# Folding constant as four 32-row products, rings of 4, and the 64-unit product on two column groups

## What is computed

```python
k = key_param @ Wk + bk ; v = k @ Wv + bv            # 32 patterns only
A = sparsemax((query @ Wq + bq) . k / sqrt(32))      # per head, over 32 patterns
attn = transpose(A @ v, (0, 2, 1, 3)).reshape(B, L, H*D) @ Wo + bo
x = layernorm(query + attn)
s = x @ Win + bin_                                   # 512 -> 64
h = relu(s[..., None] * W1 + b1)                     # 64 x 16
g = einsum('btmh,mh->btm', h, W2) + b2
x = layernorm(x + g @ Wout + bout)
```

## Time and profile before

| | us |
|---|---|
| median of 3 runs | 1581.36 (1575.73 to 1583.24) |
| the profiled execution | 1570.85 |
| its span, first to last instruction | 1569.1 |
| PE busy in the span | 1415.4 (90%) |
| ACT busy | 1105.0 (70%) |
| DVE busy | 1096.9 (70%) |
| POOL busy | 655.8 (42%) |
| mean share of PE's full clock granted | 0.96 |

### The profile page before, as it was taken

The page is one execution under the profiler, slowest core; times in us unless marked ns, Lnnn a source line. Parts: engine busy times, 40 slices in busy tenths (PEclk is TensorE's granted clock), DMA queues, the critical chain, the costliest instruction groups (busy, mean ns, idle before and its releaser), DMA issues. The chain is left out here.

```text
span 1569.1 us, 25895 instructions
## 1 busy us (share of the span) xinstructions
PE 1415.4 (90%) x6102; PEld 915.1 (58%) x6102; DVE 1096.9 (70%) x4547; ACT 1105.0 (70%) x2402; POOL 655.8 (42%) x1645
## 2 busy tenths in 40 slices
PE   6887388799999999999999999999999999889984
PEld 5444144466666666666666666666666666545542
DVE  2654754578877877878788777888778777834454
ACT  3443143367787887788887787878888878867784
POOL 1221022223454444545544554444544444544444
PEclk9998698899999999999999999999999999989995
DMA  4333033655555555455545555555545555446753
GB/s 133 124 104 97 27 108 108 187 183 162 169 189 189 186 179 177 165 189 189 188 157 174 189 172 172 176 189 189 182 174 177 175 189 189 162 162 232 251 157 72
DMA packets 91798, 258.50 MB, mean 165 GB/s; under 512 B 15651, under 2 KB 15651, under 8 KB 75206
## 3 DMA queue, kind: packets, MB, share of 16 engines
q1 hardware_dynamic: 91590, 256.39, 49.0%
HBM read 206.00 MB, written 50.33 MB: 163 GB/s over the span
## 5 line engine op out<-in xcount | busy, mean ns | idle before, releaser
L610 PE MATMUL bank<-G_sb,pT 128*128 128x512 f32 x1024 | 465.7, 598 | 0.0
L977 DVE MAX8 top<-bank 128x8 f32<-128x32 f32 x2048 | 212.5, 181 | 146.9 <-issue 124.3
L610 PEld LDWEIGHTS bank<-G_sb,pT 128*128 128x128 f32 x1024 | 186.7, 192 | 186.9 <-issue 186.9
L419 POOL TENSOR_TENSOR shift_sq<-sum,per_row_sq 128x1 f32<-128x1 f32 x256 | 99.8, 390 | 413.1 <-DVE y_sb L883 412.8
L1019 DVE SCALAR_TENSOR_TENSOR acc<-hinge,w2c,acc 128x512 f32<-128x512 f32 x224 | 167.3, 747 | 61.3 <-ACT hinge L721 54.3
L721 ACT ACTIVATE hinge<-s_sb,b1c,w1c 128x512 f32<-128x512 f32 x256 | 205.7, 807 | 0.0
L706 ACT ACTIVATE unread<-y_sb,shift_sq 128x512 bf16<-128x512 f32 x256 | 183.1, 715 | 24.9 <-POOL minus_mean L421 24.8
L540 PE MATMUL bank<-A_hi,xT_hi 128*128 128x512 f32 x512 | 200.5, 392 | 0.0
L541 PE MATMUL bank<-A_lo,xT_hi 128*128 128x512 f32 x512 | 200.4, 391 | 0.0
L542 PE MATMUL bank<-A_hi,xT_lo 128*128 128x512 f32 x512 | 200.1, 391 | 0.0
L444 POOL TENSOR_TENSOR side<-side 128x256 bf16<-128x256 bf16 x128 | 86.6, 676 | 240.8 <-ACT side L793 240.8
(11 more groups left out here) (122 smaller groups left out, 2644.2 us busy)
## 6 DMA issues: line engine op xcount, KB each, us to landing
G_sb<-G_of_heads SPq DMA_DIRECT2D x128, 1024.0 KB, 5.4
x_sb<-in_L_attn_query_dram SPq DMA_DIRECT2D x128, 256.0 KB, 4.7
y_sb<-in_L_attn_query_dram SPq DMA_DIRECT2D x256, 128.0 KB, 5.4
out_dram<-o_sb SPq DMA_DIRECT2D x256, 128.0 KB, 4.7
G_of_heads<-y_sb SPq DMA_DIRECT2D x64, 256.0 KB, 2.6
y_sb<-in_L_attn_Wk_dram SPq DMA_DIRECT2D x1, 1024.0 KB, 5.6
y_sb<-in_L_attn_Wq_dram SPq DMA_DIRECT2D x1, 1024.0 KB, 8.2
y_sb<-in_L_attn_Wv_dram SPq DMA_DIRECT2D x1, 1024.0 KB
```

Source lines behind the costliest of these rows:

```text
L419: nc.gpsimd.tensor_tensor(shift_sq[:, par:par + 1], total[:, par:par + 1], per_row_sq[:], ALU.mult).then_inc(s_mean, 1)
L610: mm = nc.tensor.matmul(o_ps[i % 2][:], pT[:, bass.ds(pair_place(turn, i) + (i % H * C + c) * P, P)], G_sb[:, i % GR, c, :], start=(c == 0 ...
L977: mx = nc.vector.max(top8[:, h, :], z_ps[i % 2][:, h * S:(h + 1) * S])
```

## The change

1. `XR` and `OR`, the rings of `x_sb` and `o_sb`, go from 2 to 4 buffers.
2. The folded constant is built from `V_rep` instead of `V_blk`: each head's `v` repeated four times side by side, with no zeros around it. A unit of four pieces (a = 0 to 3) takes partitions 32a to 32a+31 of `VT_rep` and of `Wo_sb` and writes bank a: four 32-row matmuls, each on its own 32 rows of the array. A piece now serves four heads (32 of its 128 rows for each), so its store goes to four places in `G_dram`. There are four pieces to a slot, in slots 1 to 16, and one `bo` matmul for every sixteen pieces. In slot 0, 16 matmuls against 32 columns of the identity replace the 16 transposes, and one ACT copy the four. POOL loses two fills and the second fill of `first_place`.
3. The 64-unit product streams its 128 tokens as two halves of 64: for each chunk one product into partitions 0 to 63 (tokens 0 to 63) and one into partitions 64 to 127 (tokens 64 to 127) of the bank. ACT writes four 64 x 64 pieces instead of two of 64 x 128. `bin_sb` is loaded twice.

```diff
-        XR, YR, OR, UR, HR = 2, 16, 2, 8, 2
+        XR, YR, OR, UR, HR = 4, 16, 4, 8, 2
...
-            k = 3 * (turn * UNROLL + j - 1) if isinstance(turn, int) else PIECES
-            return range(max(k, 0), max(min(k + 3, PIECES), 0))
+            unit = turn * UNROLL + j - 1
+            return range(HPC * unit, HPC * unit + HPC) if 0 <= unit < PIECES // HPC else range(0)
...
                 for k in pieces(turn, j):
-                    h, c = k // C, k % C
+                    heads, c, a = piece(k)
                     sp.wait_ge(s_Gev, k + 1)
-                    sp.dma_start(G_dram[h, :, c * D:(c + 1) * D], y_sb[:, k % STAGES, :]).then_inc(
-                        s_Gst[k % STAGES], 16)
+                    sp.dma_start(G_dram[HPC * heads:HPC * heads + HPC, a * S:(a + 1) * S, c * D:(c + 1) * D],
+                                 y_sb[:, k % STAGES, :]).then_inc(s_Gst[k % STAGES], 16)
...
                     for c in range(C):
-                        mm = nc.tensor.matmul(ys_ps[0:M, 0:P], Win_sb[:, c, :], yT[:, c, :], start=(c == 0),
-                                              stop=(c == C - 1))
+                        for t in range(2):
+                            tokens = slice(t * HALF, (t + 1) * HALF)
+                            mm = nc.tensor.matmul(ys_ps[t * M:(t + 1) * M, 0:HALF], Win_sb[:, c, :],
+                                                  yT[:, c, tokens], start=(c == 0), stop=(c == C - 1))
...
-                    if c == 0:
-                        nc.tensor.matmul(G_ps[k % C][:], first_place[:], bo_row[:], start=True, stop=False)
-                    nc.tensor.matmul(G_ps[k % C][:], VT_blk[:, h, :], Wo_sb[:, c, :], start=(c > 0),
-                                     stop=True).then_inc(s_Gmm, 1)
+                    with_bo = c == 0 and a == 0
+                    if with_bo:
+                        nc.tensor.matmul(G_ps[a][:], ones_row, bo_row[:], start=True, stop=False)
+                    nc.tensor.matmul(G_ps[a][:], VT_rep[rows, heads * P:(heads + 1) * P], Wo_sb[rows, c, :],
+                                     start=not with_bo, stop=True).then_inc(s_Gmm, 1)
...
-                    for half in (slice(0, M), slice(M, P)):
-                        nc.scalar.activation(s_sb[half, par, q * P:(q + 1) * P], ys_ps[0:M, 0:P], ACT.Identity,
-                                             bias=bin_sb[:]).then_inc(s_sc, 1)
+                    for t in range(2):
+                        for half in (slice(0, M), slice(M, P)):
+                            rows = slice(t * M, (t + 1) * M)
+                            nc.scalar.activation(s_sb[half, par, q * P + t * HALF:q * P + (t + 1) * HALF],
+                                                 ys_ps[rows, 0:HALF], ACT.Identity,
+                                                 bias=bin_sb[rows, :]).then_inc(s_sc, 1)
```

More of the change, by code:

```diff
@@ L151, in build_kernel @@
         G_sb = sb("G_sb", [P, GR, C, D])
-        V_blk, VT_blk = (G_sb[:, r].rearrange("p c n -> p (c n)").rearrange("p (h n) -> p h n", h=H)
-                         for r in range(2))
+        V_rep, VT_rep = G_sb[:, 0].rearrange("p c n -> p (c n)"), G_sb[:, 1, 0, :]
         G_dram = nc.dram_tensor("G_of_heads", [H, P, C * D], F32, kind="Internal").ap()
@@ L158, in build_kernel @@
         bo_row = sb("bo_row", [1, D])
-        first_place = sb("first_place", [1, P])
+        ones_row = sb("ones_row", [1, P])[:]
         Win_sb = sb("Win_sb", [P, C, M])
@@ L163, in build_kernel @@
         bout_rows = sb("bout_rows", [P, D], F32R)
-        bin_sb = sb("bin_sb", [M, 1])
+        bin_sb = sb("bin_sb", [P, 1])
         w1c = sb("w1c", [P, KH])
@@ L288, in pieces, with piece @@
         def pieces(turn, j):
-            k = 3 * (turn * UNROLL + j - 1) if isinstance(turn, int) else PIECES
-            return range(max(k, 0), max(min(k + 3, PIECES), 0))
+            unit = turn * UNROLL + j - 1
+            return range(HPC * unit, HPC * unit + HPC) if 0 <= unit < PIECES // HPC else range(0)
+        def piece(k):
+            return k // (HPC * C), k // HPC % C, k % HPC
         def group_of(turn, i):
             return turn * (UNROLL // GROUP) + i // GROUP
-        KEY_LOADS, Q_LOADS, WLOADS = 3, 2, 16
-        FILLS = 15 + S
-        CONSTS = FILLS + 5
+        KEY_LOADS, Q_LOADS, WLOADS = 3, 2, 17
+        FILLS = 13 + S
+        CONSTS = FILLS + 4
         @block.sync
@@ L322, in _ @@
                     (Wout_sb[half, :], Wout),
+                    (bin_sb[half, :], bin_.rearrange("(m a) -> m a", a=1)),
                     (w1c[half, :], W1[:, j * KH:(j + 1) * KH]),
@@ L350, in slot @@
                     if isinstance(turn, int) and base + i < H:
-                        if h < GR:
+                        if h == 0:
                             sp.wait_ge(s_Gmm, PIECES)
-                        for k in range(C * h, C * h + C):
-                            sp.wait_ge(s_Gst[k % STAGES], 16 * (k // STAGES + 1))
+                        if h % HPC == 0:
+                            for r in range(STAGES):
+                                sp.wait_ge(s_Gst[r], 16 * (h // HPC + 1) * (HPC * C // STAGES))
                     if not isinstance(turn, int) or base + i >= GR:
@@ L592, in slot @@
                     if not isinstance(turn, int) or base + i >= 1:
-                        pe.wait_ge(s_sc, 2 * (base + i))
+                        pe.wait_ge(s_sc, 4 * (base + i))
                     for c in range(C):
@@ L635, in slot @@
                     nc.tensor.matmul(f_ps[:], acc_lo[:, here], Wout_hi[:], start=False, stop=True).then_inc(s_f, 1)
[L636 to L642, removed]
-                for k in pieces(turn, j):
-                    h, c = k // C, k % C
-                    if c == 0:
[L646 to L651, removed]
-                        nc.tensor.matmul(G_ps[k % C][:], first_place[:], bo_row[:], start=True, stop=False)
-                    nc.tensor.matmul(G_ps[k % C][:], VT_blk[:, h, :], Wo_sb[:, c, :], start=(c > 0),
-                                     stop=True).then_inc(s_Gmm, 1)
+                if turn == 0 and j == 0:
+                    for h in range(H):
+                        mm = nc.tensor.matmul(G_ps[0][:, h * S:(h + 1) * S],
+                                              V_rep[:, h * P:(h + 1) * P],
+                                              ident[:, 0:S], start=True, stop=True)
+                    mm.then_inc(s_vT, 1)
+                for k in pieces(turn, j):
+                    heads, c, a = piece(k)
+                    rows = slice(a * E, (a + 1) * E)
+                    pe.wait_ge(s_vTc, 1)
+                    if k >= HPC:
+                        pe.wait_ge(s_Gev, k - HPC + 1)
+                    with_bo = c == 0 and a == 0
[3 more added lines that the diff above has]
+                                     start=not with_bo, stop=True).then_inc(s_Gmm, 1)
             slots(pe, slot)
@@ L671, in _ @@
                     act.wait_ge(s_const, CONSTS)
[L672 to L675, removed]
+                    nc.scalar.copy(V_rep.rearrange("p (h a d) -> p h a d", h=H, a=HPC),
+                                   ps[:].rearrange("p (h d) -> p h d", h=H).unsqueeze(2).broadcast_to(
+                                       [P, H, HPC, E])).then_inc(s_sev, 1)
                 elif name == "WqT":
@@ L804, in slot @@
                 probabilities(turn, j, 1)
[L805 to L810, removed]
+                if turn == 0 and j == 0:
+                    act.wait_ge(s_vT, 1)
+                    nc.scalar.copy(VT_rep, G_ps[0][:]).then_inc(s_vTc, 1)
                 for k in pieces(turn, j):
@@ L814, in slot @@
                         act.wait_ge(s_Gst[k % STAGES], 16 * (k // STAGES))
-                    nc.scalar.copy(y_sb[:, k % STAGES, :], G_ps[k % C][:]).then_inc(s_Gev, 1)
+                    nc.scalar.copy(y_sb[:, k % STAGES, :], G_ps[k % HPC][:]).then_inc(s_Gev, 1)
             slots(act, slot)
```

11 lines of the change are left out of this document (3 added, 8 removed).

## The result

The changed kernel took 1608.67 us (median of 4 runs, 1608.30 to 1609.86), the kernel before 1582.30 on the same occasions: 1.0171 times as long, 95% interval 1.0135 to 1.0208. It is slower by 26 us, where 46 us faster was forecast, and outside the range of 1488 to 1600. The profiled execution (1608.63, span 1606.8) is 37.7 us longer than the one before.

The account below looks back on a forecast made before the run. PE was taken to bound the steady part and drain, a round trip from pieces to load the fill. The terms summed to -46 us on the profiled 1570.85, 1525; forecast against the median 1535 us, range 1488 to 1600.

Parts of the forecast that it names:

- Slots 17 to 22, -30: Fill slots that lose their pieces: round trip gone, 6.5 us a slot instead of 11.4; -30 us, bounds -35 and -15.
- The wait before slot 23, -6: The 6.65 us wait for a tile load goes because that tile is loaded earlier; -6 us (0 to -7).
- Slots 1 to 16, 0 with bounds of -10 and +30: Fill slots with four pieces instead of three: overlapped passes offset by an extra copy and store; 0 us.
- The sign that the text had named: End of the fill: a first big matmul later than 265 us, instead of 290.7, would show the forecast wrong.
- The 32-row passes: Pieces in slots 1 to 16: +19 us if loads are exposed one by one, -16 if neighbours overlap.
- The store of the output, -12: ACT's wait for the `o_sb` buffer goes with four buffers; PE's idle time comes back, -12 us (0 to -26).
- The 64-unit product, 0, with -49 as the rival: Product in each slot: 16 half passes gain 0 us; rival, column groups run in pairs, -49 on PE, chance 0.24.
- ACT's copies, +5: Four copies instead of two, 0.32 us each: fits the steady part, lengthens PE's waits in the drain; +5 us (0 to +16).
- the drain, -3: At the end DVE's 46.9 us wait for `o_sb` goes, but PE's work remains; -3 us (0 to -15).
- Slot 0, put at nothing within 2 us: First slot: 32 passes for 16 and POOL's dropped fills were put at nothing, within 2 us.
- The cold fill: Rival: less PE work in the fill lowers its clock, eight more slow slots cost 26 us; 1561 us, chance 0.14.
- The rival that ends slower: Product's weight loads show, slots 26 to 153: 1591 us (mild form, chance 0.14) or 1649 us (full form, 0.07).

Follow-up runs that it names:

- fold_fixed: The changed kernel with each piece's store written with its 32 rows, not the 4 heads, as slowest dimension: 1464.54 us, 0.9242 of before.
- rings_only: The kernel before with only the rings of `x_sb` and `o_sb` raised to 4 buffers: 1524.29 us, 0.9624 of before.
- product_only: The kernel before with only the 64-unit product on two column groups and ACT's four copies: 1595.36 us, 1.0071 of before.
- early_x: fold_fixed with tile loads issued two slots earlier, ahead of the pieces' stores in SP's order: 1419.43 us, 0.8968 of before.

## Why the prediction was wrong

By its own steps:

- *Slots 17 to 22, -30.* Right in mechanism, 24.1 measured (44.4 us, 7.4 a slot). Slots 18 to 20 and 22 took 5.3 to 6.7 us, near the 6.5 I had taken; slot 17 took 8.8 and slot 21 12.4.
- *The wait before slot 23, -6.* The wait went, but the term was counted twice: the wait ends where slot 23 begins, at 289.77, so it lies within the 68.6 us of the term above. The two together gave 24 of the 36.
- *Slots 1 to 16, 0 with bounds of -10 and +30.* **This is the step that failed**: slots 1 to 16 lost 145 us. I costed "one more ACT copy and one more store in the round trip ... 0.5 each" from the time that SP needs to issue a store, and took the transfer itself over unchanged. But the store's shape was part of the change: four heads' blocks of 32 rows in the diff, where it had been 128 rows in one. Four stores on 4 engines take 10 us, where in fold_fixed, with 16 engines, a store lands 2.7 us after its issue, and the load that PE waits for is queued behind them. Once the shape is known to leave 4 of 16 engines, the DMA rows of the kernel before give the price: three stores and a load have 64 small packets and run at up to 427 GB/s; a quarter of that is 107, and 1.05 MB then take 10 us, where the load used to land in 3.7: some 6 us more a slot, 100 us in sixteen, and already outside the bound of +30. Measured were 8.4 more from issue to next slot, 134 us in all. The sign that the text had named came too: the first big matmul starts at 415.3 us, not before 265.
- *The 32-row passes*, within that step, were cheaper than either bound: all four pieces run at once, eight passes in 1.14 us with their drain, 0.29 us a piece, where I had taken 0.53 a piece at the least. It brought nothing: with the store mended the load is issued no earlier (6.1 us after the slot's start in the median, 5.5 before), since it still stands behind the copies and four stores.
- *The store of the output, -12.* Right in mechanism, its size was off: rings_only gives 59 us against before, 0.35 us in each steady slot and the rest around it, above all after slot 127. I had bounded it by PE's idle time in two rows, 5.9 and 6.8 us. PE's other idle time went as well, such as 8.7 us for DVE (L577); that ACT's lateness had spread to DVE is my reading, no run shows it by itself. The window had the whole of it: PE went from 192.85 to 200.00 us busy in 200, and 7.15 in 200 is 0.37 us a slot, 47 us in 128.
- *The 64-unit product, 0, with -49 as the rival.* The rival was right: 9.86 to 9.46 us a slot, 0.40 against the 0.38 worked out for pairs. My argument against it, that 16 loads of 0.055 us need 0.88 us on one path, fell: loads for two column groups run at the same time, as the records show: they start in pairs 6 ns apart, each 0.138 us long, a pair every 0.058 us. The rule of the Trainium skill that I weighed there ("TensorE: Matmul & The Clock Gate", Part 3, The mechanism) would have exposed the loads; for column groups these records do not agree with it. That the product needed the ring to be worth anything (product_only, +0.7%) was in the text as "the cover is the 2 us that part 4 gives back", and the run confirms it.
- *ACT's copies, +5, and the drain, -3.* 307 ns a copy against 320. PE's wait for them rose from 11.0 to 17.8 us in all, as forecast, and the stretch from slot 127 gained 9.8 us with all parts where the rings alone gained 16.1, so the copies' +5 was about right. The drain's own -3, bounded at -15, was too small.
- *Slot 0, put at nothing within 2 us.* Wrong by little: 3.5 us longer in the changed kernel, 5.2 in fold_fixed, since 32 passes replace 16.

The cold fill, a rival, was seen (0.67 over 189 us) but as an effect: with the store mended the same passes run at 0.98 in slot 6. Over slots 0 to 16 the clock is then 0.78, below the 0.86 of before, and this costs slots 1 to 16 nothing that can be seen (183.6 us against 183.1). The rival that ends slower had its price in the weight loads and named the wrong place. Without the one step, the sum of the four stretches is 1570.85 - 24 - 78 - 10 = 1459, and fold_fixed measured 1464.5; its slots 0 to 16 took 5.6 us more than before, 5.2 of it in slot 0, which is the difference.

## What to carry to other kernels

When a change gives a DMA another shape, cost the transfer and not its issue: look at the slowest dimension of both sides, and at the count of small packets per transfer in the DMA view. A dimension of 4 in front left a quarter of the bandwidth here and also delayed the load that was queued behind it. And a gain on the bounding engine may need its cover first: here the ring of the output buffer made the shorter product worth 0.40 us a slot, and without the ring it was a loss. When a wait goes, bound the gain by the whole idle time of the engine that bounds (one minus its busy share), not by the rows that name the wait.

## What the runs showed of the hardware that was not expected

- Two column groups work at the same time with their weight loads: 16 passes of 64 columns, half of them per group, take 0.61 us from start to the next group's start, against 1.02 for 8 passes of 128. The order matters: with one group's passes all first, 0.89, and even then the second group's passes begin among those of the first.
- Four 32-row fp32 passes on the four row groups start 6 to 7 ns apart, their loads too: the eight passes of four pieces take 1.14 us including the drain (fold_fixed's slots and early_x alike), where six passes of three 128-row pieces took 2.84.
- A pass of 32 columns can cost as much as one of 128: at a granted clock of 0.54 to 0.63, 32 passes of 32 columns take 5.41 and 6.24 us (slot 0 of the changed kernel and of fold_fixed), 16 of 128 columns take 2.78.
